# A token mixer and an expert layer on one core: the table of sines from products of powers, x turned in pairs, seven low parts of weights on TensorE

## The reference

```
Bu     = einsum('btd,nd->btn', ln(x), B_w)                  # 64 states
eig    = (1 - i*omega) / (1 + i*omega)                      # on the unit circle, omega from a_params
h      = real( causal convolution of Bu with eig**t )       # t = 0..511, by FFT in the reference
x1     = x + ln( einsum('btn,dn->btd', h, C_w) + D * ln(x) )
xe     = ln(x1)
cw     = softmax(xe @ w_router) * softmax(xe @ w_gating / 0.1), normed to sum 1    # 8 experts
ffn    = sum over e of cw[e] * ( (silu(xe @ w_gate[e]) * (xe @ w_up[e])) @ w_down[e] )   # 512 wide
result = x1 + ln(ffn)
```

## Time and profile before

| | us |
|---|---|
| median of 3 runs | 1112.43 (1112.18 to 1113.23) |
| the profiled execution's own time | 1113.27 |
| its span | 1111.4 |
| TensorE busy | 1094.8 |
| unit 0 begins on TensorE | 26.54 |

### The profile page before, as it was taken

The page is one execution under the profiler, slowest core; times in us unless marked ns, Lnnn a source line. Parts: engine busy times, 40 slices in busy tenths (PEclk is TensorE's granted clock), DMA queues, the critical chain, the costliest instruction groups (busy, mean ns, idle before and its releaser), DMA issues.

```text
span 1111.4 us, 16965 instructions
## 1 busy us (share of the span) xinstructions
PE 1094.8 (99%) x4833; PEld 896.1 (81%) x4833; DVE 941.4 (85%) x1815; ACT 744.6 (67%) x1435; POOL 719.2 (65%) x886
## 2 busy tenths in 40 slices
PE   8899999999999999999999999999999999999997
PEld 5777888888888888888888888888888888888886
DVE  7999898897988979788897988979788897987866
ACT  5786676757667586676757667586676757666553
POOL 2785766748567575766748567575766748556454
...
GB/s 138 132 87 9 117 48 96 76 35 100 39 105 66 73 74 36 115 48 96 76 32 103 39 105 67 71 76 43 107 48 96 76 32 102 39 95 48 47 50 20
DMA packets 182285, 79.66 MB, mean 72 GB/s; under 512 B 124560, under 2 KB 160048, under 8 KB 182192
## 3 DMA queue, kind: packets, MB, share of 16 engines
q1 hardware_dynamic: 182192, 78.57, 26.5%
...
## 4 chain that ended last, share of the span: by engine, by line
PE 88%; issue 0%; POOL 0%; DVE 0%; POOLq 0%; ACT 0%; DVEq 0%; ACTq 0%
PE u L396 10%; PE g L397 10%; PE g L396 10%; PE u L397 10%; PE y L397 10%; PE y L396 10%; PE g L398 10%; PE u L398 10%; PE y L398 10%; PE n_ps L485 0%; PE n_ps L486 0%; PE m_ps L464 0%; PE m_ps L463 0%; PE m_ps L457 0%; PE m_ps L458 0%
## 5 line engine op out<-in xcount | busy, mean ns | idle before, releaser
L1500 POOL TENSOR_TENSOR hid_lo<-hid,hid_hi 128x512 fp32r<-128x512 f32 x256 | 341.0, 1332 | 306.6 <-ACT hid_hi L781 306.1
L775 ACT ACTIVATE gate<-g 128x512 f32<-128x512 f32 x512 | 306.0, 598 | 313.6 <-PE g L398 312.8
L1115 DVE TENSOR_TENSOR hid<-gate,u 128x512 f32<-128x512 f32 x512 | 348.0, 680 | 145.7 <-ACT gate L775 110.0
L781 ACT ACTIVATE hid_hi<-hid 128x512 fp32r<-128x512 f32 x512 | 319.6, 624 | 20.0 <-DVE hid L1115 19.3
L1124 DVE TENSOR_TENSOR hid_lo<-hid,hid_hi 128x512 fp32r<-128x512 f32 x256 | 218.4, 853 | 0.2
L396 PE MATMUL u<-xe_hi,w_hi 128*128 128x512 f32 (+1 forms) x516 | 201.0, 389 | 2.9 <-DVE hid L1115 2.7
L396 PE MATMUL g<-xe_hi,w_hi 128*128 128x512 f32 (+1 forms) x516 | 200.4, 388 | 0.3 <-DVE xe_lo L1251 0.3
L397 PE MATMUL g<-xe_lo,w_hi 128*128 128x512 f32 (+1 forms) x516 | 200.1, 388 | 0.0
L397 PE MATMUL u<-xe_lo,w_hi 128*128 128x512 f32 (+1 forms) x516 | 200.0, 388 | 0.0
L398 PE MATMUL u<-xe_hi,w_lo 128*128 128x512 f32 (+1 forms) x516 | 199.9, 387 | 0.0
L398 PE MATMUL g<-xe_hi,w_lo 128*128 128x512 f32 (+1 forms) x516 | 199.9, 387 | 0.0
...
## 6 DMA issues: line engine op xcount, KB each, us to landing
cw_b<-cw_scratch SPq DMA_DIRECT2D x128, 256.0 KB, 3.4
...
```

What stands on the lines that cost most here:

```text
L775: nc.scalar.activation(gate[:, k % 2, :], g_ps[k % 2][:], ACT.Silu).then_inc(gate_ready, 1)
L781: nc.scalar.activation(hid_hi[:, slot(c, k), :], hid[:, slot(c, k), :], ACT.Copy).then_inc(hi_ready, 1)
L1115: nc.vector.tensor_tensor(hid[:, slot(c, k), :], gate[:, k % 2, :], u_ps[k % 2][:], ALU.mult).then_inc(hid_ready, 1)
L1500: nc.gpsimd.tensor_tensor(hid_lo[:, slot(c, k), :], hid[:, slot(c, k), :], hid_hi[:, slot(c, k), :].bitcast(f32), ALU.subtract).then_inc(l ...
```

## The change

**The table of sines.** `low` holds powers 1 to 16 (not 32) and a third row with the sine's opposite sign, so that a doubling is three instructions, not four; the norming of power 4 is prepared beside the doubling and has two steps in a row, not four. Then three squarings of all 17 columns at once give powers of 16, a fourth gives (by halves of the partitions) what the cosine rows and the sine rows need, and 256 columns of `trig` are made at once as 16 x 16 products: two multiplications and a sum. The second half of the table is made later in the same way, from coarse powers turned by `c_far`, `s_far`.

**x in pairs.** ScalarE norms tiles 0, 1 and signals, then 2, 3; the turned x is copied and projected in halves of 256 columns. On TensorE the low part of piece 0 moves ahead of the turning of x; `keep_warm` gives 5 matmuls, not 7.

**Seven low parts.** TensorE makes those of pieces 0 to 6; GpSimd makes 17, at other k. Each piece is loaded when its own predecessor in the slot is split, and waited for by itself. In front of unit 0, TensorE waits for all seven of its own low parts.

**Other moves.** In the tables, the steps of the first chunk's mixer work from `merge` on come one unit later, the expert weights' (`products`, `weights`) one unit later, the second chunk's `stats_x` two later. Chunk 1's norm of y is no longer applied by ScalarE: VectorE does scale and residual in one pass over PSUM (four of 128 x 128) and the constant shift of each token is kept in `y_shift` and added at the end.

```diff
-AHEAD = 3
+PE_PIECES = 7
+STEP = 16
-FIRST_X_AT = {..., "lo_x": 5, "bu": 7, "move_b": 7, "merge": 7, "enter_cos": 8, "enter_sin": 8, "scan": 9,
-              "leave": 10, "move_sines": 11, "fold": 11, "hi_w": 12, "lo_w": 12, "c": 14, "y": 15}
+FIRST_X_AT = {..., "lo_x": 5, "bu": 7, "move_b": 7, "merge": 8, "enter_cos": 9, "enter_sin": 9, "scan": 10,
+              "leave": 11, "move_sines": 12, "fold": 12, "hi_w": 13, "lo_w": 13, "c": 15, "y": 16}
-FIRST_OWN_AT = {"softmax": 1, "peak": 2, "silus": 3, "exps": 4, "products": 5, "weights": 6, "weigh": 10}
+FIRST_OWN_AT = {"softmax": 1, "peak": 2, "silus": 3, "exps": 4, "products": 6, "weights": 7, "weigh": 11}
-WARM = 7
-LATE_SPLITS = (3, 4, 5, 6, 7, 8, 9, 10, 11, 13, 14, 15, 19, 21, 22)
+WARM = 5
+LATE_SPLITS = (3, 4, 5, 6, 7, 9, 11, 13, 14, 15, 17, 19, 21, 23, 25, 26, 27)
...
+            def wait_staged(e, i):
+                n = PIECES * (e - 2) + i
+                if 0 <= n < PE_PIECES:
+                    sp.wait_ge(w_lo_act, n + 1)
+                elif n >= PE_PIECES:
+                    sp.wait_ge(w_lo_done, n + 1 - PE_PIECES)
...
-            early_turn_x()
             pe.wait_ge(minus_ready, 1)
             make_lo(0)
-            early_bu()
+            early_turn_x((0, 1))
+            early_turn_x((2, 3)).then_inc(xn_turned, 1)
+            early_bu(FIRST_HALF)
+            early_bu(SECOND_HALF).then_inc(bu_ready, 1)
             make_lo(1)
-            make_lo(2)
             pe.wait_ge(diag_ready, 1)
             early_skip((0, 1))
             pe.wait_ge(w_half, 1)
             early_c((0, 1)).then_inc(y_half_made, 1)
+            make_lo(2)
             make_lo(3)
...
-            pe.wait_ge(w_lo_act, 8)
+            pe.wait_ge(w_lo_act, PE_PIECES)
...
-            early_norm_x()
             round_piece(0, 0)
+            act.wait_ge(x_shift, 1)
+            early_norm_x((0, 1))
+            early_norm_x((2, 3))
+            keep_lo(0)
+            act.wait_ge(xn_turned, 1)
+            early_copy_x(FIRST_HALF)
+            early_copy_x(SECOND_HALF)
             round_piece(0, 1)
-            early_copy_x()
...
+            last = low[:, 1:3, :]
+            for level in range(3):
+                nxt = coarse[level % 2]
+                nc.vector.tensor_tensor(squares, last, last, ALU.mult)
+                if level == 0:
+                    early_shift_x()
+                links[0] += 1
+                nc.vector.scalar_tensor_tensor(out=nxt[:, 1], in0=last[:, 1], scalar=2.0, in1=last[:, 0],
+                                               op0=ALU.mult, op1=ALU.mult).then_inc(trig_link, 1)
+                dve.wait_ge(trig_link, links[0])
+                then(nc.vector.tensor_tensor(nxt[:, 0], squares[:, 0], squares[:, 1], ALU.subtract))
+                last = nxt
...
+            def products(t):
+                nc.vector.tensor_tensor(square(part_a), coarse_by(t, 0), fine_by(1), ALU.mult)
+                return nc.vector.tensor_tensor(square(part_b), coarse_by(t, 1), fine_by(2), ALU.mult)
+
+            then(products(ahead))
+            nc.vector.tensor_tensor(trig[:, FIRST_HALF], part_a, part_b, ALU.add).then_inc(trig_half, 1)
...
             leave(FIRST_HALF).then_inc(w_half, 1)
-            dve.wait_ge(trig_link, links[0] + 1)
-            nc.vector.scalar_tensor_tensor(out=trig[:, SECOND_HALF], in0=trig[:, FIRST_HALF], scalar=co,
-                                           in1=v_sin[:, FIRST_HALF], op0=ALU.mult, op1=ALU.add).then_inc(trig_ready, 1)
+            dve.wait_ge(trig_link, links[0])
+            then(products(steps_a))
+            nc.vector.tensor_tensor(trig[:, SECOND_HALF], part_a, part_b, ALU.add).then_inc(trig_ready, 1)
...
             def first_residual():
-                dve.wait_ge(z_ready, 1)
-                nc.vector.tensor_tensor(x1[:, 1], x_sb[:, 1], x1[:, 1], ALU.add).then_inc(x1_ready, 1)
+                dve.wait_ge(rstd_ready, 6)
+                shifts(y_shift[:, 1], mv, rstd).then_inc(shift_ready, 1)
+                for j in range(NT):
+                    last = nc.vector.scalar_tensor_tensor(out=x1[:, 1, j, :], in0=n_ps[:, j * P:(j + 1) * P],
+                                                          scalar=rstd[:, j:j + 1], in1=x_sb[:, 1, j, :],
+                                                          op0=ALU.mult, op1=ALU.add)
```

255 lines of the change are left out of this document (126 added, 129 removed).

## The result

The changed kernel takes **1115.11 us** (median of 20 runs, 1113.60 to 1118.47) against 1112.97 us for the kernel before beside it (20 runs, 1112.06 to 1116.96). The ratio is 1.0019, 95% interval 1.0011 to 1.0027: slower, by 0.2%. The forecast was 1109.3 us, and 1115.11 lies outside its range. The profiled execution took 1113.79 us (span 1112.0), one of its shortest; that of before took 1113.27 (span 1111.4).

What follows compares the result with a forecast made beforehand. The time was taken as the head, chunk 0's waits of 5.4 us and a fixed rest with TensorE fully busy. Terms -1.6 - 1.7 + 0.2 = -3.1 us gave 1109.3 us from the median; range 1106.8 to 1111.9 us.

Steps and rivals of the forecast that it cites:

- head: Stretch up to unit 0: earlier table and projection start unit 0 at 24.9 us, not 26.54; -1.6 us.
- units 5 to 17: Chunk 0's waits of TensorE for VectorE: part of them leaves as work moves; -1.7 us of 3.71.
- units 17 to 31: Late units: more GpSimd splits against spread VectorE work; +0.2 us, between -1.2 and +3.
- two fewer low parts on TensorE cost and give nothing by themselves: Head: TensorE has slack there, so making fewer low parts was priced at nothing.
- rival A: Chunk 0's waits are only moved, VectorE being full, and late pieces cost 0.7 us more; 1111.1 us, chance 0.22.
- GpSimd's two pieces fewer in units 3 to 11: Chunk 0: seven GpSimd pieces, not nine, each costing VectorE up to 1.1 us where they meet; by halves 1.1 us saved.
- the fold: Chunk 0: a VectorE operation of 0.67 us that leaves the stretch, counted as 0.6 us saved.
- 0.7 us for piece 22: Unit 28: GpSimd's low part of the weights (expert 7's up) comes 1.4 us late, half of it counted.
- 0.5 us back for spreading VectorE's work: Late units: residual, statistics and merge spread over units 20 to 22 remove part of 1.65 us of waits; -0.5 us.
- Rival C: Late units: GpSimd's late pieces hold everything; +3.2 us in sum, 1115.6 us, slower; chance 0.06.
- Loads cost nothing: Expert 2's reload falls under the head, chunk 2's x has some 4 us of cover; both priced at nothing.
- Rival B: TensorE idles ahead of unit 0 and its clock falls as unit 0 starts, costing 1.5 us; 1110.8 us, chance 0.12.

Runs made afterwards that it cites:

- e5: Kernel before with the load of x of chunk 3 and later ahead of y's store and reload; 1111.58 us, ratio 0.9989.
- e4: Changed kernel with the load of x of chunk 3 and later ahead of y's store and reload; 1113.01 us, ratio 1.0000.
- r2: The kernel before, unedited, one more execution; span 1111.4 us.
- r1: The changed kernel, unedited, run again; 1114.74 us, ratio 1.0021.
- e3b: Changed kernel's head alone, with the kernel before's unit tables, load order and pieces (9 low parts on TensorE, 15 on GpSimd); 1112.05 us, ratio 0.9998.
- e6: e3b with the load of x of chunk 3 and later ahead of y's store and reload; 1111.30 us, ratio 0.9984.
- e7: e6 with the changed kernel's unit tables; 1111.40 us.
- e2: Changed kernel with the expert weights' steps back in units 5, 6 and 10; 1114.38 us, ratio 1.0012.
- e14: e4 with the expert weights' steps back in units 5, 6 and 10; 1112.18 us, ratio 0.9995.
- e8: e4 with the kernel before's unit tables; 1115.11 us.
- e9: New head with the kernel before's unit tables, 7 low parts on TensorE, 17 on GpSimd, all in units 2 to 22; 1111.54 us, ratio 0.9989.
- e13: e11 with the expert weights' steps back in units 5, 6 and 10; 1110.53 us, ratio 0.9986.
- e1: Changed kernel with five late GpSimd pieces split earlier, the last in unit 24; 1115.47 us, ratio 1.0023.
- e10: e4 with three GpSimd pieces moved from units 23, 25 and 26 to 22, 23 and 24; 1113.31 us, ratio 1.0009.
- e11: e4 with 8 low parts on TensorE and 16 on GpSimd, in units 3 to 22; 1110.70 us, ratio 0.9984.

## Why the prediction was wrong, step by step

e5 and e4 are the kernel before and the changed one with x's load out of the way and the clock at 1.00 in both heads; their marks give each step of the sum a measured value:

| step | forecast | measured, e4 less e5 |
|---|---|---|
| head | -1.6 | 24.58 - 25.25 = -0.67 |
| units 5 to 17 | -1.7 | 53.21 - 53.21 = 0 (units 0 to 22) |
| units 17 to 31 | +0.2 | 19.63 - 17.18 = +2.45 (units 22 to 29) |
| sum | -3.1 | +1.8 (spans 1111.2 and 1109.4), medians +1.43 |

**The head** was right in its order of steps, and wrong in its base and in one price. Shift 8.60 (8.5 forecast), half the table at 12.25 (12.0), enter 12.70 with VectorE waiting for TensorE and the table done before (13.1), y's statistics 15.98 (16.35), unit 0 24.60 (24.9). The projection took 1.10 us at a clock of 1.00, not the 1.91 us forecast at 0.50. The gap to the earlier trace rows is 1.94 us, more than forecast. But 1.1 us of it was the lower clock of the earlier trace rows, which the old head has in some executions and not in others, and 0.17 us that x was turned later in that execution. The prediction read the 0.50, took 1.91 us for the projection with it, and ended "at full clock it would be half", without asking whether before's 26.54 us would then stand. With both heads at the lower clock the gap is 1.27 us (r2 26.36, r1 25.09), with neither 0.67. How often each clock stands in the runs behind the medians isn't on record.

The wrong price is "two fewer low parts on TensorE cost and give nothing by themselves". With nine of them the new head starts unit 0 at 25.3 us (e3b, e6, e7), where the old one at full clock starts it too (25.25), because TensorE has no idle time left; with eight or seven it is 24.5 to 24.6. So at full clock the new table and the pairs give nothing at unit 0 unless TensorE makes a low part less. Fewer low parts under the old head were not run; there unit 0 waited 0.41 us for VectorE's `xe_lo` (e5).

**Units 5 to 17, -1.7 us**: failed in the sum, as rival A (the waits only move) had it, though not by A's reason that nothing was to be had. `act_lo`'s wait went as forecast, and `pr` takes 0.18 us at its new place, not 1.28. The prediction gave the weights' new place no price at all: there they stand in GpSimd's burst of splits, two of their operations cost 1.24 and 1.03 us instead of 0.15 and 0.19, and with the statistics of x behind them they hold `hid` of unit 8 for 2.4 us. Put back (e2, e14), the wait of 1.3 us returns and the stretch is 1.2 us shorter: most of the forecast gain was there, and the change gave it away. The rows had shown both halves of this, 1.28 us for a `pr` of 32 columns and what GpSimd was doing at such a time.

The largest term of the -1.7 us, -1.1 for GpSimd's two pieces fewer in units 3 to 11, isn't there with the old tables. TensorE turns y of chunk 1 40.44 us after unit 0 with nine pieces (e6), 40.51 us with seven (e8) and 40.47 us with ten from unit 2 on (e9). TensorE in e6 and e8:

```profile
65.78 0.66 PE L412 MATMUL n_ps<-ident,y_sb 128*128 128x128 f32 x4 [0.37 <-DVE y_sb L1017]
```

```profile
65.09 0.65 PE L412 MATMUL n_ps<-ident,y_sb 128*128 128x128 f32 x4 [0.37 <-DVE y_sb L1009]
```

With the new tables and the weights put back it may be: units 0 to 22 take 53.08 us with nine (e13) and 52.03 with seven (e14), but these two differ in the late pieces and the loads as well. No run shows the 0.6 us of the fold by itself.

**Units 17 to 31, +0.2 us**: the step that failed most, and it turned the sign. The prediction's centre was 0.7 us for piece 22 and 0.5 us back for spreading VectorE's work. The trace shows 1.76 us for piece 22, some 0.5 more ahead of the logits and 0.35 for xn, and e7 shows 0.3 us for the spreading. Rival C had the mechanism, with a chance of 0.06, and the prediction set against it that the pieces "would have to meet nearly every time". They do: with the last piece in units 24 to 27 (changed, e1, e8, e10) the scan took 2.3 us each time, with the last in unit 22 (before, e7, e9, e11) 1.22, though what it waited behind was GpSimd's own `hid_lo`, pushed there by a split. e7 shows that without late pieces the whole 2.4 us is gone. Rival C's count of two meetings at 1.1 us was near the two seen, 1.13 us on the low part and 1.09 on the scan; its piece 22 at 95.8 us was not, it came at 92.40.

**"Loads cost nothing"** held for expert 2 and chunk 2. For chunk 3 nobody asked: x's load behind y's reload costs both kernels, the kernel before 1.2 us in its median (e5; its first profile showed a wait of 0.4 us), the changed one 1.7 to 2.1 (1114.74 and 1115.11 against e4). So of the 2.1 to 2.7 us measured between them 1.4 are the schedule, and 0.7 to 1.3 this load. Why it is late more often or for longer in the changed kernel isn't settled; its y store starts 0.6 us later, and beyond that no run here tells.

**Rival B** (the clock falls as unit 0 starts) was wrong in place: it held at 1.00 through both idle times of 1.11 and 0.69 us ahead of unit 0. It did fall behind the 2.41 us wait at 48 us, in some executions (the first profile, r1, e7, e11); there it cost nothing, since TensorE then waited for `acc` 0.94 us instead of the 2.51 it waited in e4, and both reached 55.7 us. The two warm-up matmuls fewer were run only together with the rest of the new head, so that they cost nothing isn't shown. The speed of y's residual in chunk 1, read from PSUM, can't be told apart from the rest of e7's 0.3 us.
